# Row maxima for a softmax shift: moved by single-element DMAs instead of matmuls with an identity

## The chip, the cores and the metric

The kernel runs on one core of a Trainium2 chip. The time is that of one execution on the device, in microseconds (us). Engines are named as in the profile: PE (TensorE, matmuls), PEld (its weight loads), DVE (VectorE), ACT (ScalarE), POOL (GpSimd), SP (SyncE, which here only issues DMAs). A name with a q (ACTq, SPq) is the engine's sequencer, the part that walks through the instruction list, waits on semaphores and issues DMAs.

## What is computed

One decoder layer on `x` of 8 batches x 512 tokens x 256 features, in three parts, each followed by a residual and a layer norm: a chunked linear attention, a cross attention with 16 heads of 64 over a context of 512 tokens, and a feed-forward with ternary weights. The change lies in the cross attention:

```python
qw = (q_in @ Wq + bq).reshape(B, M, HEADS, QSIZE)
kw = (k_in @ Wk + bk).reshape(B, N, HEADS, QSIZE)
vw = (v_in @ Wv + bv).reshape(B, N, HEADS, KSIZE)
a = jnp.einsum('bmhd,bnhd->bhmn', qw, kw) / jnp.sqrt(jnp.float32(QSIZE))
a = jnp.where(key_mask[:, None, None, :], a, -jnp.inf)
a = jax.nn.softmax(a, axis=-1)
o = jnp.einsum('bhmn,bnhd->bmhd', a, vw).reshape(B, M, HEADS * KSIZE)
```

The softmax subtracts the largest score of each query before the exponential.

## The kernel before

The heads are taken two at a time, so a batch has 8 pairs and the loop 64 pairs, numbered `g`; `p` is the pair's number within its batch. Tokens are cut into 4 tiles of 128. Head 0 of a pair lies on partitions 0 to 63, head 1 on 64 to 127, and matmuls of the two run side by side on PE. The scores are wanted with keys on the partitions, because they are the input of the product with the values. But the maximum that has to be subtracted runs over keys, so the kernel first computes the scores a second time, roughly, with queries on the partitions (`max_scores`), and DVE takes each query's negated maximum over the 512 keys (`negated_maxima`). The result is one number per query, lying down the partitions: a column of the tile `nmx` for each query tile and head. To be added to scores with keys on the partitions, it has to lie along a row.

That is done in two steps. `maxima_to_row` (line 1264) multiplies `nmx`, which is zero but for the two columns 0 and 64 of each query tile, by the identity, four matmuls of 128 x 128, into the bank `ROW`; this gives a tile with the maxima of head 0 in row 0 and of head 1 in row 64. `shift_row` (line 1002) lets ACT copy that bank to the tile `shift`. In `key_scores` (line 1245) the fourth matmul of each key tile multiplies `shift` by ones, which adds the row to all 128 keys. The two other terms of a score (high and low parts of queries and keys) are the three matmuls before it.

Each engine has its list for a pair written out by hand, and semaphores tie the lists together; in the steady part they run as follows.

- **PE** (`batch`, line 1313): scores of key tile 0 of pair g, first maxima tile of pair g+1, then tiles 1, 2, 3 likewise; products with the values for key tiles 0 and 1; the softmax denominators of pair g-1 (`sums`, which come after the wait for the fourth exponential of pair g); products for key tiles 2 and 3; the wait for all eight maxima of pair g+1 and its row matmuls; keys and queries of pair g+2. After pair 0 and pair 4 of a batch an output projection of half the heads follows (24 matmuls), after pair 7 the values of the next batch (48 matmuls).
- **ACT** (line 1030): four exponentials (`exps`, line 969, of 1,024 columns each), in pair 6 the rounding of the next batch's `x`; the reciprocal of the denominators of pair g-1 in two steps (lines 990 and 992); the copy of the product with the values (`pvc`, 984); `shift_row` for pair g+1; `att_hi` of pair g-1 (1000); `k_hi` and `q_hi` of pair g+2 (1008 and 1012). These two are the high parts that PE reads; their low parts are made by DVE.
- **DVE** (line 1162): the eight maxima of pair g+1 (line 1118; the read-out of the accumulator is the short instruction behind each), in pair 6 and 7 the mask preparations; two steps on the reciprocal and the normalisation of pair g-1 (1123, 1125, 1131), `att_lo` (1136), `k_lo` (1141), `q_lo` (1146).
- **POOL** (line 936): adds the probabilities of the four key tiles and splits the sum into high and low 16-bit parts for `sums`.
- **SP** (line 855): loads and stores of whole batches, once per batch.

PE starts the first maxima tile of pair g+2, which is in its list right behind the first key tile of pair g+1, only when `q_hi` of pair g+2 is there.

```python
        def shift_row(g):
            act.wait_ge(row_ps, g + 1)
            act.activation(shift[:], ROW, ACT.Copy).then_inc(row_out, 1)
```

Of the kernel before, what the change touches and what calls it, by code (L numbers as in the profile page):

```python
# [16 lines left out]
ACT = mybir.ActivationFunctionType  # L17
# [59 lines left out]
def decoder_layer(nc, a, out):  # L77
    x1_dram = nc.dram_tensor("x1_scratch", [D, B * T], F32, kind="Internal").ap()
    y2_dram = nc.dram_tensor("y2_scratch", [D, B * T], F32, kind="Internal").ap()
    with ExitStack() as whole:  # L80
# [8 lines left out]
        c["ones_w"] = sb(whole, "ones_w", [P, P], F32)  # L89
        c["ident"] = sb(whole, "ident", [P, P], F32R)  # L90
        c["eps"] = sb(whole, "eps", [P, 1], F32)
# [168 lines left out]
def linear_attention_phase(block, ctx, sb, named_sem, a, c, ps, x1_dram):  # L260
# [34 lines left out]
    stage = c["raw"][:].rearrange("p k i t -> p k (i t)")  # L295
    ident_f = sb(ctx, "ident_f", [P, P], F32)
    bits = sb(ctx, "bits", [P, 6, P], F32)
# [36 lines left out]
    def _(sp):  # L334
# [9 lines left out]
        load_weight("WvT", w_in)  # L344
        sp.dma_start(ident_f[:], a["ident"]).then_inc(consts_in, 16)
        sp.dma_start(bits[:], a["bits"]).then_inc(consts_in, 16)
# [129 lines left out]
    def _(dve):  # L476
# [24 lines left out]

        dve.wait_ge(consts_in, 32)
        dve.wait_ge(sig_done, 1)
        dve.tensor_copy(c["ident"][:], ident_f[:]).then_inc(setup, 1)
        dve.tensor_copy(dmask[:], bits[:, 5, :]).then_inc(pow_step, 1)
# [283 lines left out]
def cross_attention_phase(block, ctx, sb, named_sem, a, c, ps, x1_dram, y2_dram, la, f):  # L789
# [16 lines left out]
    junk = sb(ctx, "junk", [P, 2, 2, T], BF16)  # L806
    shift = sb(ctx, "shift", [P, T], F32R)
    sb(ctx, "spare", [P, DK, T], F32)
    v = sb(ctx, "v_b", [P, NT, HD], F32)
# [4 lines left out]
    mcol = sb(ctx, "mcol", [P, NT], F32)  # L814
    nmx = sb(ctx, "nmx", [P, NT, P], F32R)
    ones_r = sb(ctx, "ones_r", [P, P], F32R)
# [8 lines left out]
    k_ps, k_hi_out, k_lo_out = sem("k_ps"), sem("k_hi_out"), sem("k_lo_out")  # L825
    smax_ps, nm_out, row_ps, row_out = sem("smax_ps"), sem("nm_out"), sem("row_ps"), sem("row_out")
    st_ps, exp_out, pv_ps, pvc_out, acc_out = sem("st_ps"), sem("exp_out"), sem("pv_ps"), sem("pvc_out"), sem("acc_out")
# [10 lines left out]
    FIRST_KEY, FIRST_QUERY = (ps[:, 2, :], ps[:, 3, :]), (ps[:, 6, :], ps[:, 0, :])  # L838
    PV, ROW, KEY, QUERY, DEN = ps[:, 0, :], ps[:, 1, :], ps[:, 2, :], ps[:, 6, :], ps[:, 3, :]
    VAL = (ps[:, 4, :], ps[:, 5, :])  # L840
# [54 lines left out]
    def _(pool):  # L895
# [55 lines left out]

        pool.memset(f32(nmx[:]), 0.0).then_inc(consts, 1)
        pool.memset(f32(ones_r[:]), 1.0).then_inc(consts, 1)
# [4 lines left out]
        pool.tensor_copy(x_hi[:], raw_x).then_inc(x_rounded, 1)  # L958
        split_x(0)
        split_output_weight()  # L960
        batch(0, True, False)
# [5 lines left out]
    def _(act):  # L967
# [33 lines left out]

        def shift_row(g):
            act.wait_ge(row_ps, g + 1)
            act.activation(shift[:], ROW, ACT.Copy).then_inc(row_out, 1)

# [24 lines left out]
        def batch(b, first, last):  # L1030
            for p in range(PAIRS):
# [3 lines left out]
                nxt2 = not (last and p >= PAIRS - 2)  # L1035
                p2 = (p + 2) % PAIRS
                for i in range(NT):
                    exps(b, g, i, head)
                if p == PAIRS - 2 and not last:
                    round_x(b + 1)  # L1040
# [6 lines left out]
                values_copied(g, p % 2, first and p < 2)  # L1047
                if nxt:
                    shift_row(g + 1)
                if first and p == 1:  # L1050
# [26 lines left out]
        values_out(0, (6, 7))  # L1077
        shift_row(0)
        batch(0, True, False)
# [13 lines left out]
    def _(dve):  # L1093
# [14 lines left out]
        def negated_maxima(b, g, p):  # L1108
            if p == 0:
                dve.wait_ge(mask_done, b + 1)  # L1110
            for t in range(NT):
                if isinstance(b, int):
                    dve.wait_ge(smax_ps, NT * g + t + 1)
                else:
                    dve.wait_ge(smax_ps, tiles_scored)
                    dve.reg_add(tiles_scored, tiles_scored, 1)
                for h in range(2):
                    dve.tensor_tensor_reduce(junk[:, t % 2, h], SMAX[t % 2][:, h], mask[:], -1.0, -LOWEST, ALU.add,  # L1118
                                             ALU.min, nmx[:, t, h * DH:h * DH + 1]).then_inc(nm_out, 1)

# [108 lines left out]
    def _(pe):  # L1229
# [15 lines left out]
        def key_scores(g, p, kt):  # L1245
            par, cols, banks = p % 2, slice(kt * P, (kt + 1) * P), SCORE[kt % 2]
            if kt == 0:
                pe.wait_ge(k_lo_out, g + 1)
                pe.wait_ge(q_lo_out, g + 1)
                pe.wait_ge(row_out, g + 1)  # L1250
            for n, (l, r) in enumerate(((k_hi, q_hi), (k_lo, q_hi), (k_hi, q_lo))):
                for h in range(2):
                    pe.matmul(banks[:, h], l[OWN[h], par, cols], r[OWN[h], par], start=(n == 0), stop=False)  # L1253
            for h in range(2):
                mm = pe.matmul(banks[:, h], ones_r[OWN[h], :], shift[OWN[h], :], start=False, stop=True)  # L1255
            mm.then_inc(st_ps, 1)

        def max_scores(g, p, t):
# [3 lines left out]
            mm.then_inc(smax_ps, 1)  # L1262

        def maxima_to_row(g):
            pe.wait_ge(nm_out, 8 * g + 8)
            for t in range(NT):
                mm = pe.matmul(ROW[:, t * P:(t + 1) * P], nmx[:, t, :], c["ident"][:], start=True, stop=True)  # L1267
            mm.then_inc(row_ps, 1)

# [43 lines left out]
        def batch(b, first, last):  # L1313
            for p in range(PAIRS):
# [47 lines left out]
                if nxt:  # L1362
                    maxima_to_row(g + 1)
                if nxt2:
# [38 lines left out]
        pe.wait_ge(bo_centred, 1)  # L1403
        maxima_to_row(0)
        batch(0, True, False)
# [301 lines left out]
```

## Time and profile before

| what | value |
|---|---|
| time, median of 3 runs (lowest to highest) | 1361.86 us (1358.66 to 1362.01) |
| time of the profiled execution | 1363.67 us |
| its span, from first to last instruction | 1361.9 us |
| mean granted clock of TensorE | 0.979 |
| PE busy | 1303.6 us (96%), 7056 matmuls |
| PEld busy | 880.7 us (65%) |
| DVE busy | 919.2 us (67%) |
| ACT busy | 829.2 us (61%) |
| POOL busy | 771.8 us (57%) |
| DMA | 42.85 MB, 25535 packets |

The busy times count work on the engine's datapath; register, semaphore and DMA-issuing instructions are not in them. The matmuls are pipelined, so the length of one is more than the distance to the next. The attention loop takes the time from about 205 to 1155 us; the linear attention lies before it and the feed-forward behind it.

### The profile page before, as it was taken

How to read it: one execution, taken by the hardware profiler on the slowest of the kernel's cores; microseconds unless marked ns; L12 is line 12 of the kernel's file. 1: busy time of each engine (PE TensorE's matmuls, PEld its weight loads, DVE VectorE, ACT ScalarE, POOL GpSimd, SP SyncE). 2: the span in 40 equal slices, each digit the busy share in tenths (PEclk: the TensorE clock that was granted, in tenths of full speed). 3: DMA queues.
4: the chain of work that ended last, by engine and by line, in shares of the span. 5: the costliest groups of instructions: out<-in, count | busy, mean ns of one | idle time of the engine just before them, and what ended most of it. 6: DMA issues, size and time to landing. Idle time of an engine off the chain costs nothing.

```text
span 1361.9 us, 20879 instructions
## 1 busy us (share of the span) xinstructions
PE 1303.6 (96%) x7056; PEld 880.7 (65%) x7056; DVE 919.2 (67%) x1803; ACT 829.2 (61%) x1122; POOL 771.8 (57%) x447
## 2 busy tenths in 40 slices
PE   5999979999999999999999999999999998899995
PEld 4767756667566656666666666657566665577773
DVE  5678876674766676566747656674765677678885
ACT  2344436675666576665757665675666666678883
POOL 3504227885777687667948767694876787300000
PEclk8999989999999999999999999999999999899997
DMA  6211220000100100010010001000100100111100
GB/s 209 96 45 62 80 79 1 1 1 1 65 1 1 64 0 0 0 64 0 0 58 6 0 0 64 0 0 15 48 0 0 63 1 1 34 45 47 46 32 31
DMA packets 25535, 42.85 MB, mean 31 GB/s; under 512 B 3440, under 2 KB 7936, under 8 KB 25488
## 3 DMA queue, kind: packets, MB, share of 16 engines
q1 hardware_dynamic: 24672, 39.10, 8.4%
q0 software_dynamic: 816, 3.15, 0.7%
q8 instruction: 27, 0.44, 0.1%
q14 instruction: 20, 0.16, 0.0%
HBM read 29.66 MB, written 12.58 MB: 31 GB/s over the span
## 4 chain that ended last, share of the span: by engine, by line
PE 87%; DVE 4%; ACT 3%; POOL 2%; issue 2%; SPq 1%; DMA 1%; POOLq 0%; ACTq 0%; DVEq 0%
PE ps L1276 15%; PE ps L1253 14%; PE ps L48 10%; PE ps L50 10%; PE ps L49 9%; PE ps L1261 4%; PE ps L1255 4%; PE ps L1267 2%; PE ps L1309 2%; PE ps L1310 2%; PE ps L1308 2%; PE ps L1620 2%; PE ps L1621 2%; PE ps L1285 2%; PE ps L721 1%
## 5 line engine op out<-in xcount | busy, mean ns | idle before, releaser
L1118 DVE CUSTOM_DVE_ANT_0 junk<-ps,mask 128x512 bf16<-128x512 f32 x512 | 319.9, 687 | 94.2 <-PE ps L1261 92.7
L977 ACT ACTIVATE prob<-ps,mcol 128x1024 f32<-128x1024 f32 x256 | 282.1, 1116 | 138.8 <-PE ps L1255 134.8
L905 POOL TENSOR_TENSOR acc<-acc,prob 128x1024 f32<-128x1024 f32 x128 | 306.5, 2395 | 11.5
L902 POOL TENSOR_TENSOR acc<-prob 128x1024 f32<-128x1024 f32 x64 | 153.9, 2404 | 227.6 <-ACT prob L977 226.6
L1276 PE MATMUL ps<-prob,v_b 128*64 128x512 f32 x1024 | 244.5, 598 | 0.0
L919 POOL TENSOR_TENSOR acc_lo<-acc,acc_hi 128x1024 f16<-128x1024 f32 x64 | 138.9, 2170 | 5.1
L1276 PEld LDWEIGHTS ps<-prob,v_b 128*64 128x64 f32 x1024 | 67.8, 136 | 107.9 <-issue 73.6
L1123 DVE TENSOR_TENSOR ps<-ps,recip 128x512 f32<-128x512 f32 x64 | 44.8, 699 | 120.3 <-ACT recip L992 120.3
L1253 PE MATMUL ps<-q_hi,k_hi 64*128 64x512 f32 x512 | 115.2, 446 | 4.6 <-DVE rs L226 2.8
L1261 PE MATMUL ps<-k_hi,q_hi 64*128 64x512 f32 x512 | 103.1, 399 | 8.3 <-DVE nmx L1118 5.6
L1255 PE MATMUL ps<-shift,ones_r 64*128 64x512 f32 x512 | 102.6, 396 | 0.0
L1253 PE MATMUL ps<-q_lo,k_hi 64*128 64x512 f32 x512 | 102.4, 395 | 0.0
L1253 PE MATMUL ps<-q_hi,k_lo 64*128 64x512 f32 x512 | 102.4, 395 | 0.0
L990 ACT ACTIVATE recip<-ps 128x512 f32<-128x512 f32 x64 | 38.2, 597 | 84.2 <-PE ps L1285 84.2
L1253 PEld LDWEIGHTS ps<-q_hi,k_hi 64*128 64x128 f32 x512 | 48.8, 186 | 54.2 <-issue 26.9
L1136 DVE SCALAR_TENSOR_TENSOR att_lo<-ps,bv,att_hi 128x512 fp32r<-128x512 f32 x64 | 48.1, 751 | 48.7 <-ACT att_hi L1000 48.7
L1000 ACT ACTIVATE att_hi<-ps,bv 128x512 fp32r<-128x512 f32 x64 | 44.0, 688 | 43.5 <-DVE ps L1131 43.5
L1267 PEld LDWEIGHTS ps<-ident,nmx 128*128 128x128 f32 x256 | 33.9, 192 | 53.0 <-issue 53.0
L1018 ACT ACTIVATE v_b<-ps 128x512 f32<-128x512 f32 x64 | 38.1, 598 | 47.9 <-PE ps L50 47.9
L915 POOL CAST acc_hi<-acc 128x1008 f16<-128x1008 f32 x64 | 65.4, 1022 | 0.0
L1261 PEld LDWEIGHTS ps<-k_hi,q_hi 64*128 64x128 f32 x512 | 48.7, 186 | 25.5 <-DVE nmx L1118 7.2
L48 PE MATMUL ps<-cx_hi,wfc_hi 128*128 128x512 f32 x128 | 56.9, 444 | 1.2 <-DVE cx_lo L250 1.2
(213 smaller groups left out, 2972.4 us busy)
## 6 DMA issues: line engine op xcount, KB each, us to landing
x_in<-in_xT SPq DMA_DIRECT2D x8, 512.0 KB, 3.7
x_scratch<-x_a SPq DMA_DIRECT2D x8, 512.0 KB, 2.8
raw<-in_cT SPq DMA_DIRECT2D x8, 512.0 KB, 5.7
raw<-x_scratch SPq DMA_DIRECT2D x8, 512.0 KB, 4.8
y<-x_scratch SPq DMA_DIRECT2D x8, 512.0 KB, 3.8
y_scratch<-y SPq DMA_DIRECT2D x8, 512.0 KB, 2.8
y_c<-y_scratch SPq DMA_DIRECT2D x8, 512.0 KB, 4.1
outT<-x SPq DMA_DIRECT2D x8, 512.0 KB, 2.8
```

Source lines behind the costliest of these rows:

```text
L48: pe.matmul(out, lh, rh, start=(i == 0), stop=False)
L49: pe.matmul(out, lh, rl, start=False, stop=False)
L50: mm = pe.matmul(out, ll, rh, start=False, stop=(i == n - 1))
L902: pool.tensor_tensor(total, prob[:, 0], prob[:, 1], ALU.add).then_inc(acc_out, 1)
L905: pool.tensor_tensor(total, total, prob[:, kt], ALU.add).then_inc(acc_out, 1)
L919: pool.tensor_tensor(acc_lo[:], acc[:], acc_hi[:], ALU.subtract).then_inc(sum_lo_out, 1)
L977: act.activation(prob[:, i].rearrange("p h t -> p (h t)"), SCORE[i % 2].rearrange("p h t -> p (h t)"), ACT.Exp, scale=SCALE, bias=mcol[:, ...
L1118: dve.tensor_tensor_reduce(junk[:, t % 2, h], SMAX[t % 2][:, h], mask[:], -1.0, -LOWEST, ALU.add, ALU.min, nmx[:, t, h * DH:h * DH + 1]).t ...
L1253: pe.matmul(banks[:, h], l[OWN[h], par, cols], r[OWN[h], par], start=(n == 0), stop=False)
L1255: mm = pe.matmul(banks[:, h], ones_r[OWN[h], :], shift[OWN[h], :], start=False, stop=True)
L1261: mm = pe.matmul(SMAX[t % 2][:, h], q_hi[OWN[h], par, toks], k_hi[OWN[h], par], start=True, stop=True)
L1276: mm = pe.matmul(PV[OWN[h], :], v[:, kt, cols], prob[:, kt, h, :], start=(kt == 0), stop=(kt == NT - 1))
```

## The change

Eight DMAs per pair bring the maxima to the rows. `nmx` shrinks to one column per query tile and head, doubled for even and odd pairs; `shift` is doubled likewise, and is filled with zeros once, since only rows 0 and 64 are ever written. Each transfer takes 128 numbers of 4 bytes, one from each partition, and writes them next to each other in one partition. ACT issues them, four (two query tiles x two heads) after its third exponential and four after its fourth. PE waits for the transfers within `key_scores`, just before the first matmul that reads `shift`. PE's list keeps its wait for the maxima where the row matmuls stood. The identity is no longer loaded. The unused tiles `spare` and `spare_end` keep the addresses of the others as they were.

```diff
@@ -87,7 +87,6 @@
         c["ones_w"] = sb(whole, "ones_w", [P, P], F32)
-        c["ident"] = sb(whole, "ident", [P, P], F32R)
         c["eps"] = sb(whole, "eps", [P, 1], F32)
@@ -293,7 +292,6 @@
     stage = c["raw"][:].rearrange("p k i t -> p k (i t)")
-    ident_f = sb(ctx, "ident_f", [P, P], F32)
     bits = sb(ctx, "bits", [P, 6, P], F32)
@@ -342,7 +340,6 @@
         load_weight("WvT", w_in)
-        sp.dma_start(ident_f[:], a["ident"]).then_inc(consts_in, 16)
         sp.dma_start(bits[:], a["bits"]).then_inc(consts_in, 16)
@@ -499,9 +496,8 @@
 
-        dve.wait_ge(consts_in, 32)
+        dve.wait_ge(consts_in, 16)
         dve.wait_ge(sig_done, 1)
-        dve.tensor_copy(c["ident"][:], ident_f[:]).then_inc(setup, 1)
         dve.tensor_copy(dmask[:], bits[:, 5, :]).then_inc(pow_step, 1)
@@ -804,15 +800,16 @@
     junk = sb(ctx, "junk", [P, 2, 2, T], BF16)
-    shift = sb(ctx, "shift", [P, T], F32R)
-    sb(ctx, "spare", [P, DK, T], F32)
+    shift = sb(ctx, "shift", [P, 2, T], F32R)
+    sb(ctx, "spare", [P, T + 2 * P], F32)
     v = sb(ctx, "v_b", [P, NT, HD], F32)
...
     mcol = sb(ctx, "mcol", [P, NT], F32)
-    nmx = sb(ctx, "nmx", [P, NT, P], F32R)
+    sb(ctx, "spare_end", [P, NT, P - 4], F32)
+    nmx = sb(ctx, "nmx", [P, 2, NT, 2], F32R)
     ones_r = sb(ctx, "ones_r", [P, P], F32R)
@@ -823,7 +820,7 @@
     k_ps, k_hi_out, k_lo_out = sem("k_ps"), sem("k_hi_out"), sem("k_lo_out")
-    smax_ps, nm_out, row_ps, row_out = sem("smax_ps"), sem("nm_out"), sem("row_ps"), sem("row_out")
+    smax_ps, nm_out, row_in = sem("smax_ps"), sem("nm_out"), [sem("row_in_even"), sem("row_in_odd")]
     st_ps, exp_out, pv_ps, pvc_out, acc_out = sem("st_ps"), sem("exp_out"), sem("pv_ps"), sem("pvc_out"), sem("acc_out")
@@ -836,7 +833,7 @@
     FIRST_KEY, FIRST_QUERY = (ps[:, 2, :], ps[:, 3, :]), (ps[:, 6, :], ps[:, 0, :])
-    PV, ROW, KEY, QUERY, DEN = ps[:, 0, :], ps[:, 1, :], ps[:, 2, :], ps[:, 6, :], ps[:, 3, :]
+    PV, KEY, QUERY, DEN = ps[:, 0, :], ps[:, 2, :], ps[:, 6, :], ps[:, 3, :]
     VAL = (ps[:, 4, :], ps[:, 5, :])
@@ -949,7 +946,6 @@
 
-        pool.memset(f32(nmx[:]), 0.0).then_inc(consts, 1)
         pool.memset(f32(ones_r[:]), 1.0).then_inc(consts, 1)
@@ -957,6 +953,8 @@
         split_x(0)
+        pool.wait_ge(la.gate_used, B)
+        pool.memset(f32(shift[:]), 0.0).then_inc(consts, 1)
         split_output_weight()
@@ -999,9 +997,12 @@
 
-        def shift_row(g):
-            act.wait_ge(row_ps, g + 1)
-            act.activation(shift[:], ROW, ACT.Copy).then_inc(row_out, 1)
+        def maxima_to_rows(g, p, half):
+            act.wait_ge(nm_out, 8 * g + 4 * half + 4)
+            for t in (2 * half, 2 * half + 1):
+                for h in range(2):
+                    row = shift[h * DH:h * DH + 1, p % 2, t * P:(t + 1) * P]
+                    act.dma_start(f32(row), f32(nmx[:, p % 2, t, h:h + 1])).then_inc(row_in[p % 2], 16)
 
@@ -1034,8 +1035,13 @@
                 p2 = (p + 2) % PAIRS
+                pn = (p + 1) % PAIRS
                 for i in range(NT):
                     exps(b, g, i, head)
+                    if nxt and i == 2:
+                        maxima_to_rows(g + 1, pn, 0)
+                if nxt:
+                    maxima_to_rows(g + 1, pn, 1)
                 if p == PAIRS - 2 and not last:
@@ -1045,8 +1051,6 @@
                 values_copied(g, p % 2, first and p < 2)
-                if nxt:
-                    shift_row(g + 1)
                 if first and p == 1:
@@ -1075,7 +1079,9 @@
         values_out(0, (6, 7))
-        shift_row(0)
+        act.wait_ge(consts, 3)
+        for half in range(2):
+            maxima_to_rows(0, 0, half)
         batch(0, True, False)
@@ -1116,7 +1122,7 @@
                     dve.tensor_tensor_reduce(junk[:, t % 2, h], SMAX[t % 2][:, h], mask[:], -1.0, -LOWEST, ALU.add,
-                                             ALU.min, nmx[:, t, h * DH:h * DH + 1]).then_inc(nm_out, 1)
+                                             ALU.min, nmx[:, p % 2, t, h:h + 1]).then_inc(nm_out, 1)
 
@@ -1247,12 +1253,13 @@
                 pe.wait_ge(q_lo_out, g + 1)
-                pe.wait_ge(row_out, g + 1)
             for n, (l, r) in enumerate(((k_hi, q_hi), (k_lo, q_hi), (k_hi, q_lo))):
...
                     pe.matmul(banks[:, h], l[OWN[h], par, cols], r[OWN[h], par], start=(n == 0), stop=False)
+            if kt == 0:
+                pe.wait_ge(row_in[par], 16 * NT * (g - par) + 32 * NT)
             for h in range(2):
-                mm = pe.matmul(banks[:, h], ones_r[OWN[h], :], shift[OWN[h], :], start=False, stop=True)
+                mm = pe.matmul(banks[:, h], ones_r[OWN[h], :], shift[OWN[h], par], start=False, stop=True)
             mm.then_inc(st_ps, 1)
@@ -1260,12 +1267,6 @@
             mm.then_inc(smax_ps, 1)
-
-        def maxima_to_row(g):
-            pe.wait_ge(nm_out, 8 * g + 8)
-            for t in range(NT):
-                mm = pe.matmul(ROW[:, t * P:(t + 1) * P], nmx[:, t, :], c["ident"][:], start=True, stop=True)
-            mm.then_inc(row_ps, 1)
 
@@ -1360,7 +1361,7 @@
                 if nxt:
-                    maxima_to_row(g + 1)
+                    pe.wait_ge(nm_out, 8 * g + 16)
                 if nxt2:
@@ -1401,7 +1402,6 @@
         pe.wait_ge(bo_centred, 1)
-        maxima_to_row(0)
         batch(0, True, False)
@@ -1692,7 +1692,7 @@
         "uT": i["L0_ffn_u"].T, "v": i["L0_ffn_v"], "gate": i["L0_ffn_gate"].reshape(1, 1),
-        "ident": np.eye(P, dtype=np.float32), "bits": bits,
+        "bits": bits,
     }
...
     sent, aps = {}, {}

```

## Rows read from the trace of the kernel before

**Rows 1.** Windows: stretch, its us, busy us of each engine, granted clock, DMA share, GB/s.
```profile
102.00:136.00 34.00, 31.19 (x163) 25.19 (x162) 27.98 (x29) 13.71 (x18) 14.36 (x6) 1.00 0.18 62
705.34:827.07 121.73, 121.38 (x706) 78.19 (x705) 78.63 (x182) 76.49 (x98) 88.59 (x50) 1.00 0.05 18
```

**Rows 2.** Waits of PE in 225 to 1140 us: total, times, longest.
```profile
PE ps L1261 <- ACT q_hi L1012: 1.8, 6, 0.3
```

**Rows 3.** Timeline of PE, one pair and the start of the next: start, us, instruction.
```profile
717.77 0.49 PE L1253 MATMUL ps<-q_hi,k_hi 64*128 64x512 f32 x2
718.57 0.40 PE L1255 MATMUL ps<-shift,ones_r 64*128 64x512 f32 x2
...
724.54 0.39 PE L1285 MATMUL ps<-acc_hi,ones_h 128*64 128x512 f16 x2
...
726.79 0.66 PE L1267 MATMUL ps<-ident,nmx 128*128 128x128 f32 x4
727.28 0.44 PE L48 MATMUL ps<-bc_hi,wk_hi 128*128 128x512 f32 x1
...
730.17 0.50 PE L1253 MATMUL ps<-q_hi,k_hi 64*128 64x512 f32 x2
```

**Rows 4.** Timeline of ACT around the same pair.
```profile
712.85 0.60 ACT L990 ACTIVATE recip<-ps 128x512 f32<-128x512 f32 x1 [1.49 <-PE ps L1285]
...
715.08 0.60 ACT L1004 ACTIVATE shift<-ps 128x512 fp32r<-128x512 f32 x1
716.42 0.69 ACT L1000 ACTIVATE att_hi<-ps,bv 128x512 fp32r<-128x512 f32 x1 [0.74 <-DVE ps L1131]
...
721.58 2.19 ACT L977 ACTIVATE prob<-ps,mcol 128x1024 f32<-128x1024 f32 x2 [0.30 <-PE ps L1255]
```

**Rows 5.** Timeline of DVE in the same pair.
```profile
718.60 0.75 DVE L1146 SCALAR_TENSOR_TENSOR q_lo<-ps,bq,q_hi 128x512 fp32r<-128x512 f32 x1
719.37 0.69 DVE L1118 CUSTOM_DVE_ANT_0 junk<-ps,mask 128x512 bf16<-128x512 f32 x1
...
721.82 0.09 DVE L1118 DVE_READ_ACCUMULATOR2_ANT nmx<- 128x1 fp32r x1
...
724.30 0.08 DVE L1118 DVE_READ_ACCUMULATOR2_ANT nmx<- 128x1 fp32r x1
```

**Rows 6.** Timeline of SP's queue; all issues of mcol (ns shortest/median/longest).
```profile
7.20 5.49 SPq L350 DMA_DIRECT2D bT<-in_fast_bT  x1
...
13.22 0.42 SPq L352 DMA_DIRECT2D uT<-in_uT  x1
13.69 0.42 SPq L353 DMA_DIRECT2D gt<-in_gate  x1
...
L853 SPq DMA_DIRECT2D mcol_u<-in_mask_cols x8: 345/428/537, 163.7 to 954.8; - x8
```

**Rows 7.** ACT's loop branch at the end of a batch, and ACT's timeline there.
```profile
L1080 ACTq COMPARE_BRANCH  x1: 45/45/45, 809.3 to 809.3; - x1
...
809.20 0.60 ACT L1018 ACTIVATE v_b<-ps 128x512 f32<-128x512 f32 x1 [0.76 <-PE ps L50]
```

**Rows 8.** Timeline of ACT, pairs 5 and 6 of a batch; all preparations of mask columns.
```profile
767.96 0.60 ACT L990 ACTIVATE recip<-ps 128x512 f32<-128x512 f32 x1 [1.50 <-PE ps L1285]
...
779.27 1.05 ACT L1023 ACTIVATE bx_hi<-raw 128x1024 fp32r<-128x1024 f32 x1
780.87 0.60 ACT L990 ACTIVATE recip<-ps 128x512 f32<-128x512 f32 x1 [0.55 <-PE ps L1285]
...
L1106 DVE TENSOR_SCALAR mcol<-mcol_u x8: 161/1281/1439, 183.3 to 1035.8; 128x4 f32<-128x4 uint8 x8
```

**Rows 9.** Landing of the single-element transfer mcol; packets in 0.2 us of it.
```profile
DMA to landing us min/median/max: 2.9/5.0/5.7
...
DMA packets 52, 0.00 MB, mean 1 GB/s; under 512 B 52, under 2 KB 52, under 8 KB 52
```

## The prediction

> **What bounds the kernel now.** I read the windows first. One batch in the middle of the attention loop (the 121.73 us from 705.34 on) has PE busy for 121.38 us at a granted clock of 1.00, while ACT is busy for 76 us, DVE for 79 and POOL for 89 [rows 1]. So PE sets the time there, and a batch is about as long as PE's list of matmuls. The waits say the same: between 225 and 1140 us the largest wait that PE names is one of 1.8 us in total, six times, on ACT's `q_hi` [rows 2]. That row is also a warning. ACT delivers `q_hi` with almost nothing to spare, though ACT looks half idle. A share of 63% busy hides a chain that returns just in time.
>
> The timeline of one pair shows where. PE starts a pair at 717.77 and the next at 730.17, so a plain pair lasts 12.4 us. The four row matmuls start at 726.79 and the keys at 727.28: they hold PE for 0.49 us. The sums, which wait for the fourth exponential, start at 724.54 [rows 3]. On ACT the third exponential starts at 721.58 and the fourth directly behind it, and both are over at 723.77 [rows 4]: 0.77 us before PE asks. On DVE the maxima of the next pair run from 719.37 to 724.38, the fourth of the eight is out at 721.91, and `q_lo` starts at 718.60, directly ahead of the maxima [rows 5].
>
> **The change, part by part.**
>
> *Removed from PE:* 64 x 4 matmuls, 0.49 us a pair [rows 3]. PE is the bound, so this is worth up to 64 x 0.49 = 31 us if nothing else moves. PE keeps its wait for the maxima at the same place.
>
> *Removed from ACT:* one copy of 0.60 us a pair [rows 4]. It started at 715.08 and ended at 715.68, ahead of a wait for DVE that ended only at 716.42, so it cost nothing and gives nothing.
>
> *Added to ACT:* eight DMA issues a pair, four behind the third exponential (they wait for the fourth maximum) and four behind the fourth exponential (they wait for the eighth). ACT issues no DMA in this trace, so the price is bounded by SP's. Two neighbouring issues on SP that wait for nothing are 0.42 us long and start 0.47 us apart (13.22 to 13.69); the eight issues of `mcol`, which like the new transfers moves 128 pieces of 4 bytes, are 0.35 to 0.54 us long, median 0.43, so 0.40 to 0.59 apart. The far upper end is the issue at 7.20, which held SP for 5.49 us behind several megabytes of loads [rows 6]; the far lower end is a sequencer step of ACT itself, 0.04 us [rows 7]. I take 0.47, the same kind of instruction with no backlog ahead of it; four are 1.88 us.
> The Trainium skill, "DMA: Bandwidth & Descriptors", section "Issuing engines are not separate DMA queues", calls the issue time usually small relative to the DMA itself. By that rule the sum would go as in the second rival; SP's rows give 0.40 to 0.59 us for each issue, and 64 x 8 of them go into a list that has to be on time.
>
> Does an issue wait until ACT has finished the activation ahead of it? ACT's loop branch ran at 809.3, while the activation that had started at 809.20 (0.60 us long) was still running [rows 7]. So the sequencer goes on while the datapath works, and I let the first four issues run beside the third exponential. Then:
> - First four: from 721.91 + 0.05 to 723.84. The fourth exponential starts there and ends at about 724.95, the sums start at 725.0 in place of 724.54. That is 0.5 us lost on PE, and it eats the 0.49 saved. A pair that starts on time is therefore as long as before.
> - Last four: from 724.43 to 726.3, and the reciprocal estimate, `pvc`, `att_hi`, `k_hi` and `q_hi` are all queued behind them on ACT. DVE's three steps and its low parts wait for those, and DVE's next maxima wait for them in turn.
>
> This closes a loop that PE did not enter before: maxima 5.01 (719.37 to 724.38), hand-over 0.05, four issues 1.88, reciprocal estimate to `att_hi` 3.57 (712.85 to 716.42), `att_hi` to the start of `q_lo` 2.18 (716.42 to 718.60), `q_lo` to the maxima 0.77 [rows 4, 5]. The sum is 13.46 us. Without the issues it was 11.5 and hidden under PE's 12.4; now it is 1.04 us longer than the old pair.
>
> The loop is forgiven where PE has extra work: the projections (after pairs 0 and 4) and the values of the next batch (after pair 7). The pairs that follow them (1, 5, 0) start on time and come out even. Pairs 2, 3 and 4 lose 1.04 each. In pair 6 ACT also rounds `x` (1.05 us, in the same loop); that pair took 12.91 us before, from one reciprocal estimate to the next (767.96 to 780.87), and would take 13.46 + 1.05 = 14.51, so +1.60. In pair 7 DVE prepares the mask columns (1.28 us): 14.74 against 12.42, so +2.32 [rows 8]. Per batch 3 x 1.04 + 1.60 + 2.32 = 7.0 us, times 8 is 56. The last batch has neither preparation (-4); at the start, where nothing covers the transfers, four issues and a landing stand in place of four matmuls and a copy (+2). Sum: +54 us.
>
> *The landing.* The nearest transfer is `mcol`, 128 pieces of 4 bytes: 2.9 us from issue to landing at best, 5.0 in the median, where big loads run ahead of it. While it drained, 52 packets started within 0.2 us, which is 61 ns per packet and engine; eight elements and a semaphore per engine are 0.55 us per transfer, about the pace of the issues [rows 9]. The last one is issued at 725.9 and lands at 728.8, or at 730.9 by the median. It is wanted at 730.97 at the earliest (the shift matmuls come 0.80 us into a pair: 717.77 to 718.57 [rows 3]). I cost the landing at nothing; it is covered by PE's keys and queries, and past that cover each late microsecond is a whole one per pair. Once a batch, in pair 1, loads of 1.5 MB share the engines; that may cost 1 us a batch.
>
> *Small edits.* The identity and its copy go: they ran in a start-up phase that waits for larger loads, nothing. The zero fill on POOL becomes twice as large and moves behind POOL's splits, where POOL next waits for DVE's centred output weight; uncovered it costs its own length once, which I leave inside the +2. POOL's additions start up to 0.5 us later, but only the sums of the next pair need them. No queue of SP or POOL is passed. PE pauses up to 1 us in 13.4; in the window from 102 to 136 us PE idled 2.81 of 34 us and the clock stayed at 1.00 [rows 1], so I charge nothing for it.
>
> **The rivals.**
> - *An issue holds ACT's datapath* (or comes only after the running activation ends). The first four then start no earlier than the end of the third exponential, 722.7, and run to 724.6; the fourth exponential ends at 725.7, the sums start 1.2 us late, minus 0.49: +0.7 in the three even pairs, and the loop becomes about 14.2: +1.75, 1.75, 1.75, 2.35, 3.0 in the others. That is 12.7 a batch, about +100: 1462 us. Against it: the branch row [rows 7].
> - *The issue is cheap on ACT* (0.04 to 0.1 us, as its register steps). The fourth exponential is on time, the loop is 11.8, under PE's new 11.9. Pairs 6 and 7 gain little, for their preparations stand in the loop, the rest gain 0.49: about 2.4 a batch, -19 us, 1343. This is the case in which the change is faster. It decides at about 0.27 us per issue. Against it: the shortest of the eight `mcol` issues takes 0.35 [rows 6].
> - *Elements drain slowly.* At twice 61 ns per packet a transfer takes 1.1 us, the second four queue behind 2.4 us of the first, and the last lands some 9 us after the eighth maximum. The loop maxima, landing, shift matmul, first score, maxima is then about 15: +2.5 in most pairs, about +125, 1487 us. For it: nothing in this trace reads single elements of SBUF. If all 128 elements went through one engine, a transfer would take 129 x 61 ns = 7.9 us, and eight 63 us a pair: over 4000 us.
>  The Trainium skill, same page, "Rules for kernel authors", says that a non-contiguous last dimension lowers to one descriptor per element and should be rearranged; its section "Why a DMA increments its semaphore by 16 and not by 1" would spread 128 x 128 over 16 engines, which speaks against the one-engine case. No row here shows such a transfer.
> - *No change*, because an issue costs about 0.27 and the terms cancel.
>
> **How the numbers follow.** The profiled execution took 1363.67 us (span 1361.9), the median of three runs is 1361.86; I add the terms to the latter. Forecast 1361.9 + 54 = 1416. With 0.40 us per issue the loop is 13.2 and the sum +30 to +40; with 0.59 it is about +85. Chances: forecast 0.50, ACT held 0.20, slow elements 0.12 and one engine 0.04, cheap issue 0.10, no change 0.04. What a measurement can tell from no change is about 0.3%, 4 us. So slower 0.86, same 0.04, faster 0.10. The range runs from 1376 (0.35 us per issue and some terms too large) to 1500 (slow elements); it leaves out the cheap issue and the one engine.
>
> **What would show it.** Right: DMA issues on ACT's sequencer about 0.4 us long; the fourth exponential starting about 2.3 us after the third; PE waiting for `q_hi` and for the fourth exponential, close to 1 us in pairs 2, 3, 4, 6 and 7 and hardly in pairs 1 and 5; the estimate waiting no longer for PE. Wrong: issues below 0.2 us, PE still above 99% busy in the loop, or PE's wait named as a DMA that writes `shift`.

## The result and the profile after

The changed kernel takes 1466.43 us (median of 4 runs, 1465.04 to 1468.39) against 1361.62; the ratio is 1.0778 (95% interval 1.0763 to 1.0793), so it is 105 us slower. The forecast was slower by 54, and the range held the time.

The first rows of the changed kernel's page, busy time, share of the span and instructions:

```profile
span 1466.6 us, 20867 instructions
...
PE 1298.2 (89%) x6800; PEld 843.8 (58%) x6800; DVE 902.1 (62%) x1802; ACT 778.7 (53%) x1058; POOL 768.5 (52%) x447
```

PE does the same work less 256 matmuls and is busy for 89% of a longer span, where it was 96%. The share of every engine fell, which is how a loop across engines looks. ACT's busy time even fell in microseconds, from 829.2 to 778.7: the 64 copies of 0.60 us are gone, and the issues that took their place are not counted as busy. The chain that ended last counts them:

```profile
PE 45%; DVE 17%; ACTq 16%; ACT 11%; issue 8%; POOL 1%; SPq 1%; DMA 1%; POOLq 0%; DVEq 0%
ACTq L1005 16%; PE ps L48 7%; PE ps L49 7%; PE ps L50 7%; DVE junk L1124 6%; ACT prob L975 4%; PE ps L1258 3%; PE ps L1277 3%; PE ps L1311 2%; PE ps L1309 2%; PE ps L1310 2%; PE ps L1621 2%; PE ps L1620 2%; DVE ps L1129 2%; DVE ps L1131 2%
```

In the kernel before, PE was 87% of that chain. Now it is 45%, and 16% of the span are DMA issues in ACT's sequencer (ACTq), a line that did not exist.

All instructions that write or read `shift`, in ns shortest/median/longest, and the transfers' time from issue to landing:

```profile
L1005 ACTq DMA_DIRECT2D shift<-nmx x512: 476/622/1897, 200.4 to 1249.6; - x171
...
L1262 PE MATMUL ps<-shift,ones_r x512: 385/393/792, 207.0 to 1264.2; 64*128 64x512 f32 x171
L957 POOL MEMSET shift<- x1: 956/956/956, 171.2 to 171.2; 128x1024 f32 x1
...
DMA to landing us min/median/max: 1.9/2.0/6.1
```

The 512 issues have a median length of 0.62 us, where I had taken 0.47 from the start of one to the start of the next. The landing was what I had hoped for, 2.0 us in the median. PE waited for it once in the loop (0.3 us), and for 4.5 us in the very first pair, where no work covers it. PE's waits between 195 and 225 us and between 225 and 1140 us (total, times, longest):

```profile
PE ps L1262 <- DMA shift<-nmx: 4.5, 1, 4.5
...
PE ps L1286 <- ACT prob L975: 63.5, 55, 1.9
PE ps L1268 <- ACT q_hi L1013: 18.0, 27, 1.4
PE ps L1258 <- ACT prob L975: 7.9, 5, 1.7
PE ps L48 <- POOL bx_lo L920: 7.2, 7, 1.1
PE ps L1262 <- DMA shift<-nmx: 0.3, 1, 0.3
```

The row of before was 1.8 us on `q_hi` [rows 2]. It is 18.0 now, and the largest wait is a new one, 63.5 us for the fourth exponential ahead of the sums.

A plain pair on ACT, with the sequencer's issues (x4 is a burst of four):

```profile
787.28 0.69 ACT L1013 ACTIVATE q_hi<-ps,bq 128x512 fp32r<-128x512 f32 x1
...
789.56 2.35 ACT L975 ACTIVATE prob<-ps,mcol 128x1024 f32<-128x1024 f32 x2 [0.59 <-PE ps L1262]
791.38 2.43 ACTq L1005 DMA_DIRECT2D shift<-nmx  x4
793.98 1.11 ACT L975 ACTIVATE prob<-ps,mcol 128x1024 f32<-128x1024 f32 x1 [2.07 <-DVE nmx L1124]
794.07 2.43 ACTq L1005 DMA_DIRECT2D shift<-nmx  x4
796.62 0.60 ACT L988 ACTIVATE recip<-ps 128x512 f32<-128x512 f32 x1 [1.53 <-PE ps L1286]
797.25 0.63 ACT L990 ACTIVATE recip<-recip 128x512 f32<-128x512 f32 x1
797.79 0.58 ACT L982 ACTIVATE pvc<-ps 128x512 f32<-128x512 f32 x1
800.12 0.69 ACT L998 ACTIVATE att_hi<-ps,bv 128x512 fp32r<-128x512 f32 x1 [1.74 <-DVE ps L1137]
...
801.27 0.69 ACT L1013 ACTIVATE q_hi<-ps,bq 128x512 fp32r<-128x512 f32 x1
```

And on DVE and PE in the same pair:

```profile
788.83 0.68 DVE L1124 CUSTOM_DVE_ANT_0 junk<-ps,mask 128x512 bf16<-128x512 f32 x1
...
791.27 0.08 DVE L1124 DVE_READ_ACCUMULATOR2_ANT nmx<- 128x1 fp32r x1
...
793.71 0.08 DVE L1124 DVE_READ_ACCUMULATOR2_ANT nmx<- 128x1 fp32r x1
```

```profile
786.45 0.50 PE L1258 MATMUL ps<-q_hi,k_hi 64*128 64x512 f32 x2
...
795.23 0.41 PE L1286 MATMUL ps<-acc_hi,ones_h 128*64 128x512 f16 x2 [1.20 <-ACT prob L975]
...
797.50 0.50 PE L48 MATMUL ps<-bc_hi,wk_hi 128*128 128x512 f32 x1
...
800.46 0.51 PE L1258 MATMUL ps<-q_hi,k_hi 64*128 64x512 f32 x2
...
802.01 0.50 PE L1268 MATMUL ps<-k_hi,q_hi 64*128 64x512 f32 x2 [0.35 <-ACT q_hi L1013]
```

The fourth maximum is out at 791.35, the first burst runs from 791.38 to 793.81, and the fourth exponential starts behind it at 793.98, 2.1 us after ACT's datapath fell idle. The second burst starts at 794.07, 0.09 us after that exponential and beside it: an issue does not hold the datapath. It ends at 796.50, the estimate starts at 796.62, and `att_hi` 3.50 us later. (The row of the estimate still names PE's sums as what ended its wait. The last of them started at 795.46 and is about 0.4 us long, so they were over some 0.6 us before; the burst ended last.) PE starts the next pair 14.01 us after the last one, against 12.40 [rows 3].

The chain that ended last, in this pair, runs from the fourth maximum through both bursts to the estimate (start, us, what):

```profile
791.27 0.10 DVE nmx L1124
791.38 0.48 ACTq L1005
...
794.07 0.48 ACTq L1005
...
796.62 0.61 ACT recip L988
```

So eight issues stand in the loop, not the four that I had put there. That does not show in the length of this pair, because the first burst (over at 793.81) and the last four maxima (over at 793.79) run side by side and end together.

### The profile page after: what moved, and what is told of

It reads as the page before. It is cut to its first block, busy times and chain, and to the rows that moved or that the text cites. A ratio compares the mean times of both kernels' runs of the same rounds, so it can differ in the third digit from the quotient of the medians.

```text
span 1466.6 us, 20867 instructions
## 1 busy us (share of the span) xinstructions
PE 1298.2 (89%) x6800; PEld 843.8 (58%) x6800; DVE 902.1 (62%) x1802; ACT 778.7 (53%) x1058; POOL 768.5 (52%) x447
## 3 DMA queue, kind: packets, MB, share of 16 engines
q10 hardware_dynamic: 73728, 0.29, 2.7%
## 4 chain that ended last, share of the span: by engine, by line
PE 45%; DVE 17%; ACTq 16%; ACT 11%; issue 8%; POOL 1%; SPq 1%; DMA 1%; POOLq 0%; DVEq 0%
ACTq L1005 16%; PE ps L48 7%; PE ps L49 7%; PE ps L50 7%; DVE junk L1124 6%; ACT prob L975 4%; PE ps L1258 3%; PE ps L1277 3%; PE ps L1311 2%; PE ps L1309 2%; PE ps L1310 2%; PE ps L1621 2%; PE ps L1620 2%; DVE ps L1129 2%; DVE ps L1131 2%
## 5 line engine op out<-in xcount | busy, mean ns | idle before, releaser
L902 POOL TENSOR_TENSOR acc<-acc,prob 128x1024 f32<-128x1024 f32 x128 | 302.6, 2364 | 11.9 <-ACT prob L975 0.6
L1268 PE MATMUL ps<-k_hi,q_hi 64*128 64x512 f32 x512 | 106.9, 414 | 26.5 <-ACT q_hi L1013 20.4
L1286 PE MATMUL ps<-acc_hi,ones_h 128*64 128x512 f16 x128 | 26.0, 401 | 74.0 <-ACT prob L975 72.1
L1286 PEld LDWEIGHTS ps<-acc_hi,ones_h 128*64 128x64 f16 x128 | 7.3, 106 | 129.1 <-issue 98.8
```

Of the source, the lines that this page charges most:

```text
L902: pool.tensor_tensor(total, total, prob[:, kt], ALU.add).then_inc(acc_out, 1)
L1268: mm = pe.matmul(SMAX[t % 2][:, h], q_hi[OWN[h], par, toks], k_hi[OWN[h], par], start=True, stop=True)
```

## The experiments

Two theories stood against each other. **Theory A**: the price is the time of the issues in ACT's instruction list, inside the loop maxima, issues, reciprocal, `att_hi`, `k_hi`, `q_hi`, maxima. **Theory B**: the transfers themselves, 128 elements of 4 bytes each, are slow or in the way. Theory C was that an ACT list with eight issues is too long wherever they stand. Ratios are against the kernel before, in the same session.

**No transfers at all.** The kernel leaves out the subtraction of the maxima: `shift` stays zero. PE keeps its wait for the eighth maximum, also once at the start.

```diff
-                    if nxt and i == 2:
-                        maxima_to_rows(g + 1, pn, 0)
-                if nxt:
-                    maxima_to_rows(g + 1, pn, 1)
...
-            if kt == 0:
-                pe.wait_ge(row_in[par], 16 * NT * (g - par) + 32 * NT)
```

> Leaves out the transfer of the maxima altogether: no issues on ACT, no row matmuls on PE, no wait for the rows; shift stays zero, so nothing is subtracted from the scores. This is the floor of the change. If the cost lies in the issues or the landings and the removed matmuls were worth their 0.49 us a pair, it gives 1361.6 - 64 x 0.49 = 1330 us; a little more (up to 1336) if pairs 6 and 7 are held by their preparations on ACT and DVE. If something else in the edit is slow (POOL's fill, the moved tiles), it stays well above 1340.

Measured: 1336.66 us, ratio 0.9819 (0.9800 to 0.9837). A plain pair took 12.0 us. This is the floor: removing the matmuls and the copy was worth 24 us, and nothing else in the edit is slow to a degree that shows.

**Issued by SP.** The calls stand in SP's list; the store of a batch goes ahead of the issues made in pair 1, the loads behind them.

```diff
+        def batch(b, loads):
+            for p in range(PAIRS):
+                g = per_pair(b, p)
+                if p == 1:
+                    store(b - 1)
+                for half in range(2):
+                    maxima_to_rows(g + 1, (p + 1) % PAIRS, half)
+                if p == 1:
+                    load_residual(b)
+                    if loads:
+                        next_load(b + 1)
```

> The same 512 transfers, issued by SP's queue in place of ACT's; SP's loads and stores of a batch are put between them in pair 1. Theory A (issue time in ACT's list is the whole price): ACT's loop is as short as without transfers, the landing is covered, so 1333 to 1345 us. Theory B (the transfers themselves are slow, or their many packets disturb the chip): the time stays near 1466, and PE's waits name the DMA that writes shift. The length of an issue on SP also tells whether 0.61 us belongs to ACT's sequencer (SP then shows 0.43) or to this kind of transfer (SP then shows 0.6).

Measured: 1338.88 us, ratio 0.9837 (0.9820 to 0.9853). All 512 transfers are made and PE's list keeps its waits for them, at 2 us above the floor; none of PE's waits between 225 and 1140 us is for a transfer. In this kernel's rows for `shift` the issues are nearly as long as on ACT, so the length goes with this kind of transfer and not with ACT:

```profile
L875 SPq DMA_DIRECT2D shift<-nmx x512: 468/601/1832, 199.7 to 1123.3; - x171
...
DMA to landing us min/median/max: 1.9/2.0/3.8
```

Theory B falls with this run.

**Issues alone.** From the kernel without transfers, which leaves out the subtraction, ACT issues eight transfers a pair from a constant column into an unused tile. Ahead of the first of them it waits until those of the pair before have landed, which they have long done.

```diff
+                    row = scratch[h * DH:h * DH + 1, t * P:(t + 1) * P]
+                    act.dma_start(row, f32(ones_r[:, 0:1])).then_inc(row_in[0], 16)
```

> No maxima are moved and PE waits for no row, as in the kernel without transfers (1337), but ACT issues eight transfers of 128 single elements at the places of the changed kernel, from a constant column into a tile that nobody reads. It leaves out the subtraction of the maxima. Theory A: the issues alone make the whole loss, 1455 to 1470. If the landing, or PE's wait for the rows, has a part in it, the time lies below by that part.

Measured: 1466.53 us, ratio 1.0773 (1.0755 to 1.0791), the changed kernel's time to 0.1 us, though PE waits for no transfer. With the run before it this settles it: transfers without ACT's issues cost 2 us, ACT's issues with transfers that nobody waits for on PE cost 130 over the floor.

**Half from ACT, half from SP.** Head 0 from ACT, head 1 from SP.

```diff
-                for h in range(2):
+                for h in (0,):
```

> The same 512 transfers, half of them (head 0) issued by ACT at its two places, half (head 1) by SP. With none of the issues on ACT the time was 1339, with eight a pair 1466. Theory A: two issues in each of ACT's places make the loop 11.6 + 2 x 0.55 = 12.7 us against PE's 11.95, and pairs 6 and 7 lose more: 1365 to 1385. If the price were in the number of transfers and not in whose list they stand, it would be the 1339 of SP or the 1466 of the changed kernel. The instruction queue's packets, 46 in the changed kernel and 20 before, should fall back to about 20 with ACT's shorter list, and the pause of 2.4 us at the top of ACT's loop with them.

Measured: 1380.03 us, ratio 1.0134 (1.0117 to 1.0151), inside the expected 1365 to 1385. A plain pair took 12.7 us, against 12.0 with no issue on ACT and 14.0 with eight. The instruction queue's packets fell to 21, as expected, and PE's wait for the first exponentials at the top of a batch (7.9 us in the changed kernel) is not among its waits. The two engines are not quite independent: two issues of ACT beside SP's take 1.38 us here, and two issues with nothing beside them 1.13 (in the run with twos and fours below).

```profile
719.09 1.38 ACTq L1034 DMA_DIRECT2D shift<-nmx  x2
```

**Other places on ACT.** First four behind the fourth exponential, last four behind `pvc`.

```diff
-                    if nxt and i == 2:
-                        maxima_to_rows(g + 1, pn, 0)
                 if nxt:
+                    maxima_to_rows(g + 1, pn, 0)
...
                 values_copied(g, p % 2, first and p < 2)
+                if nxt:
+                    maxima_to_rows(g + 1, pn, 1)
```

> All eight issues stay on ACT, only their places change: the first four behind the fourth exponential (ACT there waited 1.5 us for the sums), the last four behind the copy pvc (ACT there waited for DVE's three steps). Theory A (what counts is that the issues stand in front of the fourth exponential and of the reciprocal estimate, in a loop with DVE): nearly all of the loss goes, 1365 to 1375 us. Theory C (an ACT list with eight issues is too long wherever they stand): 8 x 0.61 = 4.9 us a pair stay, above 1430. Theory B: near 1466.

Measured: 1378.82 us, ratio 1.0132 (1.0115 to 1.0149). The expected 1365 to 1375 was missed by 4 us, but 88 of the 105 us are gone with all eight issues still on ACT. Theory C falls. What is left above the floor, 42 us, are plain pairs of 12.6 us in place of 12.0, and waits of PE that the floor does not have: 7.8 us for the first exponentials at the top of a batch, 7.2 for the later landing, 2.8 for POOL's `bx_lo`.

**All behind the fourth exponential.**

> All eight issues behind the fourth exponential, none behind the third. The fourth exponential is on time again, PE does not wait for it before the sums. But all eight stand in front of the reciprocal estimate: the first four end at about the eighth maximum and the last four start there. If the loop through DVE's maxima and ACT's last four issues sets the pair, its length (11.6 + 4 x 0.61 = 14.0 us) does not change: 1450 to 1466 us. If the late fourth exponential was the larger part of the loss (PE waited 71 us for it), the time falls to about 1395.

Measured: 1546.34 us, ratio 1.1358 (1.1332 to 1.1383). Both expectations missed; it is 80 us slower than the changed kernel. I had kept only the last four in the loop, but one burst cannot start before the other has ended. ACT's and DVE's timeline:

```profile
705.72 3.53 ACT L975 ACTIVATE prob<-ps,mcol 128x1024 f32<-128x1024 f32 x3 [0.57 <-PE ps L1261]
...
707.45 0.08 DVE L1123 DVE_READ_ACCUMULATOR2_ANT nmx<- 128x1 fp32r x1
...
708.22 5.18 ACTq L1005 DMA_DIRECT2D shift<-nmx  x8
...
709.89 0.08 DVE L1123 DVE_READ_ACCUMULATOR2_ANT nmx<- 128x1 fp32r x1
...
713.52 0.60 ACT L988 ACTIVATE recip<-ps 128x512 f32<-128x512 f32 x1 [4.27 <-issue]
```

The eight issues take 5.2 us in a row, and the estimate waits for all of them. They start 0.69 us after the fourth maximum, behind the fourth exponential, where the first burst of the changed kernel started 0.03 us after it. So the way from the fourth maximum to the estimate is 5.99 us in place of 5.27, and a plain pair takes 14.7 us in place of 14.0. Pair 6 grows more, because the rounding of the next batch's `x` also stands behind all eight; POOL splits it only then, and PE stands still for it, 17.7 us in all:

```profile
749.28 1.06 ACT L1024 ACTIVATE bx_hi<-raw 128x1024 fp32r<-128x1024 f32 x1 [4.11 <-issue]
...
752.82 0.51 PE L48 MATMUL ps<-bx_hi,wq_hi 128*128 128x512 f32 x1 [2.97 <-POOL bx_lo L920]
```

The clock has a part in it too. These are windows of this kernel (a plain pair of 14.7 us, the next one of 16.0 us, and 3.4 us inside that one) and of the changed kernel's loop (stretch, its us, busy us of PE, PEld, DVE, ACT, POOL, granted clock, DMA share, GB/s):

```profile
670.00:684.60 14.60, 12.39 (x72) 6.91 (x72) 9.01 (x23) 7.92 (x10) 9.85 (x6) 1.00 0.04 0
684.70:700.60 15.90, 13.54 (x72) 8.15 (x72) 9.09 (x23) 7.88 (x10) 11.13 (x8) 0.89 0.04 0
688.80:692.20 3.40, 3.40 (x20) 2.65 (x18) 2.78 (x9) 1.43 (x2) 0.72 (x1) 0.50 0.00 0
```

```profile
225.00:1250.00 1025.00, 917.02 (x5110) 555.12 (x5108) 589.54 (x1395) 534.03 (x683) 674.95 (x383) 1.00 0.08 16
```

The pair in which the clock fell to 1.2 GHz for 3.4 us is 1.4 us longer than the one before it. Over the whole loop (225 to 1240 us) the mean granted clock of this kernel is 0.95; in the changed kernel's window it is 1.00. How the 80 us divide between these three was not taken apart by a run.

**The matmuls put back.**

```diff
                     pe.wait_ge(nm_out, 8 * g + 16)
+                    for t in range(NT):
+                        pe.matmul(ps[:, 1, t * P:(t + 1) * P], ones_r[:], ones_r[:], start=True, stop=True)
```

> The changed kernel with four matmuls of 128 x 128 put back on PE where the row matmuls stood (their result is read by nobody). Theory A: in most pairs PE now waits for ACT and DVE, so the 0.49 us a pair are mostly hidden: +5 to +15 us over the changed kernel, 1471 to 1481, and not 31. If PE's list still set the time, it would be +31, 1497.

Measured: 1475.51 us, ratio 1.0839 (1.0821 to 1.0858), 9 us over the changed kernel and within the expected 5 to 15. The edit puts back 252 of the 256 matmuls (not those ahead of the loop). Removed from a kernel that PE bounds, the matmuls (with ACT's copy) were worth 24 us; put into one that waits for ACT they cost 9.

**Larger pieces.** `nmx` as head by tile and `shift` with the tiles innermost, so that one transfer takes several tiles.

```diff
-                mm = pe.matmul(banks[:, h], ones_r[OWN[h], :], shift[OWN[h], par], start=False, stop=True)
+                mm = pe.matmul(banks[:, h], ones_r[OWN[h], :], shift[OWN[h], par].rearrange("p q t -> p t q"), start=False, stop=True)
```

Four transfers a pair, two in each place:

> Half as many transfers, each of 128 pieces of 8 bytes in place of 4 (both query tiles of a head at once); shift is stored with the tiles innermost and PE reads it with a stride of 16 bytes. Places as in the changed kernel, two issues and two issues. Theory A with a price per issue: 2 x 0.61 in each place, the loop falls to 12.8 us, 1372 to 1385 us. If the price goes with the bytes or pieces moved in all, the issues get longer. If PE reads a strided row slowly, the matmuls at the shift line grow beyond 393 ns.

Measured: 1399.75 us, ratio 1.0273 (1.0256 to 1.0290). Two transfers a pair, behind the fourth exponential:

> Two transfers a pair, one per head, of 128 pieces of 16 bytes, both behind the fourth exponential and the eighth maximum. Theory A: 1.2 us in the loop, 12.8 us, fourth exponential on time: 1350 to 1375 us. Landing 2.0 us after the issue is covered by PE's keys and queries.

Measured: 1399.18 us, ratio 1.0279 (1.0255 to 1.0302). Two transfers, behind `pvc`:

> As the one before, but the two issues behind the copy pvc, where ACT waits for DVE anyway. Theory A: nothing of them is left in the loop, 1332 to 1345 us, faster than both kernels; the landing (2.0 us) comes about 1 us before PE reads the row. If the landing is late, PE's waits name the DMA.

Measured: 1384.35 us, ratio 1.0160 (1.0143 to 1.0177). All three missed on the same side, and the rows for `shift` in the last one say why:

```profile
L1257 PE MATMUL ps<-shift,ones_r x512: 616/619/810, 205.9 to 1180.2; 64*128 64x512 f32 x171
L1003 ACTq DMA_DIRECT2D shift<-nmx x128: 476/582/625, 203.2 to 1170.0; - x128
```

The issues are no longer than with 4-byte pieces (the first of each two 0.48 us, the second 0.62), so between 4 and 16 bytes the price is per transfer and not per byte. But the matmul that reads the row with a stride of 16 bytes takes 619 ns where the dense row takes 393. Eight of them, two side by side, are 4 x 0.23 = 0.9 us a pair; the plain pair was 12.7 us, 0.7 over the floor, and PE's only wait in the loop was `q_hi`, 3.4 us in all. These runs bought a shorter list on ACT with a longer one on PE.

**Spread in twos and fours.** Two issues behind the third exponential, four behind the fourth, two behind `pvc`.

```diff
+                    if nxt and i == 2:
+                        maxima_to_rows(g + 1, pn, (0,))
+                if nxt:
+                    maxima_to_rows(g + 1, pn, (1, 2))
...
+                if nxt:
+                    maxima_to_rows(g + 1, pn, (3,))
```

> All eight issues on ACT as in the changed kernel, in other places: two behind the third exponential (they wait for the second maximum), four behind the fourth (sixth maximum), two behind the copy pvc (eighth maximum). Theory A: the first two end before the fourth exponential would start, the four end near the time at which ACT could start the reciprocal estimate, the last two lie in ACT's wait for DVE. With 0.55 to 0.62 us per issue 1355 to 1372 us, just about the kernel before; if an ACT list with eight issues costs 4.9 us wherever they stand, above 1430.

Measured: 1382.43 us, ratio 1.0152 (1.0135 to 1.0169), 10 us above the expected range. PE no longer waits for the fourth exponential (0.3 us in all), but the burst of four still ends about 0.5 us after ACT could have started the estimate. PE's waits are 14.7 us on `q_hi`, 8.1 for the first exponentials of a batch, 6.3 for `bx_lo` and 4.3 for a landing.

## Why the prediction was right, and where its size was off

**Right: the mechanism.** PE's gain is given back and more because the issues stand in ACT's list, in a loop with DVE. Of the marks I had set for it these were found: the issues on ACTq, the fourth exponential starting later after the third (3.2 us, where I had said 2.3), PE's waits for it and for `q_hi`, and the estimate held by something else than PE. Two were not as I had said: an issue is 0.62 us long and not 0.4, and PE waits for the fourth exponential in nearly every pair, 1.1 us in pairs 1 and 5 too, where I had said "hardly". Issues run beside an activation; the rival in which ACT's datapath is held came within 5 us of the measured time (1462) but is wrong, since the second burst starts 0.09 us into a 1.1 us exponential. Its number fitted for another reason, which only the timeline tells.

**Off: the length of an issue.** The step that failed was "I take 0.47, the same kind of instruction with no backlog ahead of it". The rows bounded it by 0.40 and 0.59; four took 2.43 us, 0.61 each. With 2.43 in the forecast's own loop it is 11.58 + 2.43 = 14.01 us, and the measured plain pair is 14.01. That the last digit agrees is luck: the other steps moved by up to 0.2 us each and cancel, and the loop has eight issues in it, of which four hide behind maxima that take just as long. Then by the forecast's rules pairs 2 to 4 lose 1.59 each, pair 6 14.01 + 1.05 - 12.91 = 2.15, pair 7 14.01 + 1.28 - 12.42 = 2.87. The pairs that start on time do not come out even any more either: four issues of 0.61 push the sums back by 1.0, which is 0.5 more than the removed matmuls give, in pairs 0, 1 and 5. That is 11.3 us a batch, 90 in all, and +88 with the same edges as before. So 34 of the 51 us by which I was short are this one term.

**The other 17 us.** This is one batch in the middle of the loop, from PE's start of a pair to its start of the next (before from 565.6 us on, after from 603.7 us on):

| pair | 0 | 1 | 2 | 3 | 4 | 5 | 6 | 7 | sum |
|---|---|---|---|---|---|---|---|---|---|
| before, us | 17.98 | 12.43 | 12.41 | 12.42 | 17.85 | 12.43 | 12.93 | 23.29 | 121.7 |
| after, us | 20.09 | 13.23 | 14.07 | 14.01 | 19.69 | 13.23 | 16.23 | 24.47 | 135.0 |
| loss | 2.1 | 0.8 | 1.7 | 1.6 | 1.8 | 0.8 | 3.3 | 1.2 | 13.3 |
| by the sum with 0.61 | 0.5 | 0.5 | 1.6 | 1.6 | 1.6 | 0.5 | 2.2 | 2.9 | 11.3 |

Two waits that the forecast left out make 15 us. In pair 6 PE now waits 1.0 us for POOL's low part of the next batch's `x` (`bx_lo`), 7.2 us in all: ACT rounds `x` in pair 6 behind both bursts, POOL splits it only then, and PE needs it for the queries. I had said of that rounding only that it stands in the loop, and not asked who waits for its result. In pair 0 PE waits for the first exponentials at the top of a batch, 7.9 us in all (5 times, up to 1.7). Small differences in the other pairs come to about 1 us more a batch. Against that stands pair 7, where the sum takes 1.7 us too much. The forecast had put DVE's preparation of the mask columns into the loop, but DVE does it while it waits for the reciprocal, with 1.86 us to spare:

```profile
722.54 0.93 DVE L1112 TENSOR_SCALAR mcol<-mcol_u 128x4 f32<-128x4 uint8 x1 [1.33 <-ACT prob L975]
725.33 0.70 DVE L1129 TENSOR_TENSOR ps<-ps,recip 128x512 f32<-128x512 f32 x1 [1.86 <-ACT recip L990]
```

So the forecast had a term too much as well, and part of its misses cancel.

ACT's first exponential at the top of a batch:

```profile
738.86 0.60 ACT L1019 ACTIVATE v_b<-ps 128x512 f32<-128x512 f32 x1 [0.76 <-PE ps L50]
741.84 2.12 ACT L975 ACTIVATE prob<-ps,mcol 128x1024 f32<-128x1024 f32 x2 [2.38 <-PE ps L1262]
```

PE had finished its first scores by 739.95, 1.9 us before, and the maxima were no condition. The changed kernel's page has 46 packets of instruction loads on one queue:

```profile
q14 instruction: 46, 0.38, 0.1%
```

Before, that queue had 20, with half the issues on ACT it had 21, and every kernel with eight issues a pair on ACT had 46; one of the packets falls between 739 and 740 us, inside this pause. The pause comes only where ACT's loop jumps back to its top (batches 2 to 6, 2.2 to 2.5 us idle) and not where it is entered (batch 1, 0.75 us), in all six kernels with eight issues on ACT and in none of the others. That ACT's longer loop body has to be loaded at its top fits all of this. It was not tested by itself.

**Right: the landing.** 73728 packets on ACT's queue for 512 transfers are 144 each, 128 elements and 16 semaphore writes. The Trainium skill, "DMA: Bandwidth & Descriptors", says in "Rules for kernel authors" of a non-contiguous last dimension that it lowers to one descriptor per element, and in "Why a DMA increments its semaphore by 16 and not by 1" that such a transfer (128 by 128) is spread over 16 engines; the packet count agrees with both. Its sentence in "Issuing engines are not separate DMA queues", that the time on the sequencer is usually small relative to the DMA itself, does not carry over to this size: the issue is 0.61 us, the landing 2.0 us, and the first holds up whatever stands behind it in ACT's list, while the second holds up nobody who has other work. The same section says that starting DMAs on several engines saves only this time on the sequencer. The run with SP agrees: here it is the whole difference, 1338.9 against 1466.4.

## What to carry to other kernels

Price a DMA as two things: the landing, which other work can cover, and the issue, which is an instruction in somebody's in-order list. With eight issues of 0.6 us a pair on ACT, which is half idle by its busy time, this kernel is 8% slower than before; with the same issues on SP, whose list had room, it is 1.6% faster (interval 1.5% to 1.8%). Before putting anything into a "half idle" engine, find the loop that returns just in time (a small wait of the bounding engine on it is the sign) and ask at which place in its list it really waits for something: there the same eight issues cost 42 us over the floor and not 130. And count everything between two waits, not only what comes last: a burst that hides behind other work in one order stands open in another, which is a part of the 80 us that the run with all eight behind the fourth exponential lost on top.

## What the runs showed of the hardware that I had not expected

- The first issue of a burst takes 0.48 us, each one directly behind it 0.62 (shortest and median of the 512; on SP 0.47 and 0.60). Eight `mcol` issues from HBM with as many pieces had 0.35 to 0.54 in the kernel before.
- Two issues on ACT took 1.13 us alone and 1.38 us beside issues on SP.
- Issues with pieces of 4, 8 and 16 bytes cost the same. The medians are 0.62, 0.58 and 0.58 us, but in bursts of four, two and two, so the shorter first issue counts for more in the last two; the shortest is 0.48 us in all three.
- A moving operand read with a stride of 16 bytes takes 619 ns for 512 columns where a dense one takes 393.
- Waits of PE up to 1.9 us, one or two in a pair, left the granted clock at 1.00 in the changed kernel's loop from 225 to 1140 us. In the run with all issues behind the fourth exponential PE stood still for 2.97 us ahead of 752.82 us, and the clock was at its lower level, 1.2 GHz, from 753.7 to 757.1 us.
- Six kernels with a longer instruction list on ACT had a pause at the top of its loop (2.2 to 2.5 us of idle ahead of the first exponential, against 0.75 before). What it waits for there is argued, not shown.
